# Full attention: rows in pairs from both ends, router groups of scattered tiles, masked value sums at the front of a batch

## The reference

```python
q, k, v = jnp.split(jnp.einsum('bsd,df->bsf', x, W), 3, axis=-1)
scores = jnp.einsum('bqd,bkd->bqk', q, k) / jnp.sqrt(jnp.float32(d_k))
scores = jnp.triu(scores, k=0)
scores = jnp.where(scores == 0, MASK_NEG, scores)
attn = jax.nn.softmax(scores, axis=-1)
return jnp.einsum('bqk,bkd->bqd', attn, v)
```

## Time and profile before

| | us |
|---|---|
| median of three runs | 1553.63 |
| lowest and highest of them | 1550.43, 2271.89 |
| time of the profiled execution | 1557.52 |
| its span, first to last instruction | 1555.8 |
| PE, DVE, ACT, POOL busy | 1285.8, 1052.4, 905.6, 778.7 |
| full attention, from its first projection to the last x | 1056.6 to 1315.1 |
| rest of the second routing, up to its last slots | 1315.1 to 1334.4 |

### The profile page before, as it was taken

The page is one execution under the profiler, slowest core; times in us unless marked ns, Lnnn a source line. Parts: engine busy times, 40 slices in busy tenths (PEclk is TensorE's granted clock), DMA queues, the critical chain, the costliest instruction groups (busy, mean ns, idle before and its releaser), DMA issues. The chain is left out here.

```text
span 1555.8 us, 34583 instructions
## 1 busy us (share of the span) xinstructions
PE 1285.8 (83%) x9684; PEld 1011.7 (65%) x9684; DVE 1052.4 (68%) x3673; ACT 905.6 (58%) x2301; POOL 778.7 (50%) x812
## 2 busy tenths in 40 slices
PE   3999999999999999999963888809978885288890
PEld 2677766766776666766743888805765665288890
DVE  7566877878777776877754555566886788355563
ACT  2677768777776776767642444406765664144450
POOL 3566676685866768567562444500022422435451
PEclk9899999999999999999985999959998998599996
DMA  8999990000000000000013122130000000121215
GB/s 255 210 207 207 208 167 8 4 12 1 15 0 6 10 0 15 0 7 8 0 56 108 56 60 59 45 108 1 1 14 15 25 16 16 45 58 57 62 54 162
DMA packets 129396, 91.89 MB, mean 59 GB/s; under 512 B 9115, under 2 KB 122030, under 8 KB 128992
## 3 DMA queue, kind: packets, MB, share of 16 engines
q1 hardware_dynamic: 118080, 71.84, 21.6%
q0 software_dynamic: 9248, 16.94, 3.3%
q10 hardware_dynamic: 1920, 1.60, 0.3%
HBM read 30.86 MB, written 61.64 MB: 59 GB/s over the span
## 5 line engine op out<-in xcount | busy, mean ns | idle before, releaser
L905 DVE CUSTOM_DVE_ANT_0 sc<-ps,mask 128x256 f32<-128x256 f32 x518 | 199.2, 421 | 159.4 <-PE ps L720 137.1
L827 ACT ACTIVATE sc<-sc,mx 128x256 f32<-128x256 f32 x516 | 256.9, 501 | 38.8 <-DVE mx L905 38.2
L1055 POOL TENSOR_TENSOR rot<-rot,sin 128x512 f32<-128x512 f32 x132 | 183.6, 1391 | 185.9 <-DVE rot L914 185.9
L1202 POOL DMA_INDIRECT yt<-yo,xt x160 | 160.4, 1002 | 197.9 <-DVE yo L1302 169.4
L534 POOL DMA_INDIRECT xg<-r_xw,r_slot x128 | 126.6, 989 | 170.0 <-DVE r_slot L511 137.9
L835 ACT COPY pT<-pt 128x512 f32<-128x512 f32 x257 | 150.1, 584 | 104.0 <-PE pt L730 95.7
L720 PE MATMUL ps<-K,Q 64*128 64x256 f32 x1036 | 193.3, 436 | 14.7 <-DVE mx L905 14.7
L1262 ACT ACTIVATE hT<-ph,b 128x256 f32<-128x256 f32 x320 | 125.4, 475 | 87.0 <-PE ph L1225 87.0
L730 PE MATMUL pt<-ident,sc 128*128 128x128 f32 x1028 | 170.7, 289 | 1.8 <-ACT sc L827 1.6
L743 PE MATMUL po<-pT,V 128*64 128x128 f32 x2048 | 170.7, 288 | 0.0
L730 PEld LDWEIGHTS pt<-ident,sc 128*128 128x128 f32 x1028 | 109.3, 142 | 86.6 <-issue 58.5
(11 more groups left out here) (235 smaller groups left out, 2730.3 us busy)
## 6 DMA issues: line engine op xcount, KB each, us to landing
xg<-zeros SPq DMA_DIRECT2D x76, 520.0 KB, 9.9
xt<-xg SPq DMA_DIRECT2D x80, 130.0 KB, 2.1
got<-yt SPq DMA_DIRECT2D x32, 256.0 KB, 4.4
yt<-yo,xt POOLq DMA_INDIRECT x160, 2.3
xg<-r_xw,r_slot POOLq DMA_INDIRECT x128, 2.3
w<-in_w SPq DMA_DIRECT2D x1, 2048.0 KB, 8.1
out_x<-x SPq DMA_DIRECT2D x8, 256.0 KB, 4.3
x<-in_hidden SPq DMA_DIRECT2D x6, 256.0 KB, 8.2
```

Source lines behind the costliest of these rows:

```text
L827: nc.scalar.activation(sc[:, b, h, :], sc[:, b, h, :], ACT.Exp, scale=-1.0, bias=mx[:, b, h:h + 1], accum_out=ls[:, c % 2, b, h:h + 1]).th ...
L905: nc.vector.tensor_tensor_reduce(sc[:, b, h, :], ps[:, h, 0:2 * P], (mask0 if b == 0 else mask)[:, :], -float(HD) ** -0.5, 3e38, ALU.add, ...
L1055: nc.gpsimd.tensor_tensor(rot[:, which, :], rot[:, which, :], s.sin[:, pos(sb)], ALU.mult).then_inc(S["pool"], 1)
L1202: nc.gpsimd.indirect_dma_start(out=s.yt, out_offset=bass.IndirectOffsetOnAxis(ap=xt[:, k, r, HID:HID + 1].bitcast(U32), axis=0), in_=yo[:, ...
```

## The change

The rows of a batch are taken in the order 0, 15, 1, 14, ..., 7, 8. A row's place in that order is r, its tile i; buffers, signals and `first` go by r, keys and x by i. A pair has five chunks. The router's groups are four tiles that are neighbours in this order (for group 0 the tiles 0, 15, 1, 14), so `Router` gets a list of tiles and ids of its own, which POOL writes with 16 `iota` instructions ahead of the stage's other work; DVE waits for them. `ROUTE_AT` becomes 11, 21, 31, 42, 51, 61, 71, 81.

The masked sums are no longer made row by row. Four matmuls of 512 columns (`a` from 12 to 15) give the column sums of all tiles of V, and DVE adds them up into `pre[:, i, :]`, one place per tile, after its first six takes. Their counts are constants set by memset. `finish` loses its add and reads `pre[:, i, :]`; `oo` gets two buffers. The scores of the first seven chunks stand between the projections and these matmuls and behind a wait for all of V. The third and fourth of the matmuls wait until DVE has read the bank (`pre` signal). The next batch's projections wait for that signal instead of the last add.

```diff
+        order = [i for k in range(BTILES // 2) for i in (k, BTILES - 1 - k)]
+        ids = m.sb("ids_b", [P, TOPK, TILES], U32)
+        rt = Router(nc, m, s, 3, 2, 0, [b * BTILES + i for b in range(BATCH) for i in order], ids)
...
-        ROUTE_AT[3], ROUTE_AT[7] = NCH + 5, 2 * NCH + 2
+        ROUTE_AT[3], ROUTE_AT[7] = NCH + 2, 2 * NCH + 1
...
-                for a in range(12):
+                for a in range(16):
...
+                    if 10 <= a < 14:
+                        pe.wait_ge(S["v"], START + 4 * b + a - 9)
+                    if a >= 14:
+                        pe.wait_ge(S["pre"], START + 4 * b + a - 13)
                     if a < 2:
-                        pe.wait_ge(S["pre_sb"], START + (BTILES - 1) * b)
+                        pe.wait_ge(S["pre"], START + 4 * b)
+                    if a == 12:
+                        pe.wait_ge(S["v"], START + 4 * (b + 1))
+                        for g in range(AHEAD):
+                            scores(g)
...
+                    elif a >= 12:
+                        g = a % 4 * SB_TILES
+                        ins = nc.tensor.matmul(pp[:, a % 2, :], s.ones[:, :], V[:, g:g + SB_TILES, 0:HID],
+                                               start=True, stop=True)
...
-                    i, c, _, _ = chunk[g]
-                    if c == 0 and i > 0:
-
-                        pe.wait_ge(S["pre_sb"], START + (BTILES - 1) * b + max(i - 2, 0))
-                        nc.tensor.matmul(pp[:, i % 2, 0:HID + 1], s.ones[:, :], V[:, i - 1, :], start=True,
-                                         stop=True).then_inc(S["pre"], 1)
...
+                def sums(a):
+
+                    dve.wait_ge(S["proj"], START + 16 * b + a + 1)
+                    for t in range(SB_TILES):
+                        i = a % 4 * SB_TILES + t
+                        if i < BTILES - 1:
+                            ins = nc.vector.tensor_tensor(pre[:, i + 1, 0:HID], pre[:, i, 0:HID],
+                                                          pp[:, a % 2, t * P:(t + 1) * P], ALU.add)
+                            ch.link(ins)
+                    dve.sem_inc(S["pre"], 1)
...
+                    nc.vector.scalar_tensor_tensor(oo[:, r % 2, :], pre[:, i, :], st[:, r % UBUF, 2:3],
+                                                   po[:, r % 2, 0:HID + 1], ALU.mult, ALU.add).then_inc(S["o"], 1)
...
                 for g in range(AHEAD - 1):
                     take(g)
+                for a in range(12, 16):
+                    sums(a)
...
+            for b in range(BATCH):
+                for k in range(TOPK):
+                    for t in range(SB_TILES):
+                        i, step = order[t], order[t + SB_TILES] - order[t]
+                        nc.gpsimd.iota(ids[:, k, bass.ds(b * BTILES + t, BTILES // SB_TILES, step=SB_TILES)].bitcast(I32),
+                                       pattern=[[step * P, BTILES // SB_TILES]],
+                                       base=(k * TILES + b * BTILES + i) * P, channel_multiplier=1).then_inc(S["ids"], 1)
```

More of the change, by code:

```diff
@@ L100 @@
     "norm1": ROUTE + " high", "experts1": EXPERT,
-    "norm2": NORM + " xT", "full": "proj qk v s copy u bias p w0 t pt pv pre pre_sb o chain tri",
+    "norm2": NORM + " xT", "full": "proj qk v s copy u bias p w0 t pt pv pre ids o chain tri",
     "norm3": ROUTE, "experts3": EXPERT,
@@ L348, with __init__ @@
     LINKS = 30
-    def __init__(self, nc, m, s, tag, bufs, primed):
+    def __init__(self, nc, m, s, tag, bufs, primed, tiles=None, ids=None):
         self.nc, self.s, self.S, self.nth, self.bufs, self.primed = nc, s, s.signals[f"norm{tag}"], tag // 2, bufs, primed
+        self.tiles, self.ids = tiles, s.ids if ids is None else ids
         small = [P, SB_TILES, EXPERTS]
@@ L1361, in full_stage @@
         block = ctx.enter_context(nc.Block())
-        chunks = [[(k, min(4, BTILES - k)) for k in range(i, BTILES, 4)] for i in range(BTILES)]
-        first = [sum(len(c) for c in chunks[:i]) for i in range(BTILES + 1)]
+        rows = [(i, [(k, min(4, BTILES - k)) for k in range(i, BTILES, 4)]) for i in order]
+        first = [sum(len(chunks) for _, chunks in rows[:r]) for r in range(BTILES + 1)]
         NCH = first[-1]
-        MARKS = 4 * BTILES + NCH
-        chunk = [(i, c, k0, n) for i in range(BTILES) for c, (k0, n) in enumerate(chunks[i])]
+        MARKS = 4 * BTILES + BTILES - 1 + NCH
+        chunk = [(r, i, c, k0, n) for r, (i, chunks) in enumerate(rows) for c, (k0, n) in enumerate(chunks)]
         def at(b, g, step):
@@ L1426, in _ @@
                     ins.then_inc(S["proj"], 1)
[L1427 to L1434, removed]
                 def turn(g):
-                    i, c, k0, n = chunk[g]
+                    r, i, c, k0, n = chunk[g]
                     pe.wait_ge(S["p"], START + NCH * b + g + 1)
@@ L1545, in _ @@
             nc.vector.memset(V[:, :, HID:], 1.0)
+            nc.vector.memset(pre[:, 0, :], 0.0)
+            for i in range(1, BTILES):
+                nc.vector.memset(pre[:, i, HID:], float(i * P))
             dve.wait_ge(S["tri"], START + 2)
+            dve.wait_ge(S["ids"], START + BATCH * TOPK * SB_TILES)
             rt.start(dve)
@@ L1595, in take @@
                                                 ALU.mult).then_inc(S["bias"], 1)
[L1597 to L1613, removed]
-                    ins.then_inc(S["o"], 1)
-                    dve.wait_ge(S["o"], START + BTILES * b + i + 1)
-                    ch.link(nc.vector.reciprocal(st[:, i % UBUF, 3:4], oo[:, HID:]))
@@ new lines, in finish @@
+                def finish(r):
+                    i = rows[r][0]
+                    dve.wait_ge(S["pv"], START + NCH * b + first[r + 1])
+                    dve.wait_ge(S["w0"], START + BTILES * b + r + 1)
+                    nc.vector.scalar_tensor_tensor(oo[:, r % 2, :], pre[:, i, :], st[:, r % UBUF, 2:3],
+                                                   po[:, r % 2, 0:HID + 1], ALU.mult, ALU.add).then_inc(S["o"], 1)
+                    dve.wait_ge(S["o"], START + BTILES * b + r + 1)
+                    ch.link(nc.vector.reciprocal(st[:, r % UBUF, 3:4], oo[:, r % 2, HID:]))
@@ L1628, in _ @@
                     route(b, g)
-                for i in range(chunk[NCH - 2][0], BTILES):
-                    finish(i)
-                assert ch.n == MARKS
+                for r in range(chunk[NCH - 2][0], BTILES):
+                    finish(r)
+                assert ch.n == MARKS, ch.n
             for g in range(NCH, NCH + MORE):
```

63 lines of the change are left out of this document (31 added, 32 removed).

## The result

The changed kernel takes 1578.3 us (median; 1577.6 to 1581.1), the kernel before 1553.2 in the same set of runs: ratio 1.0171, 95% interval 1.0151 to 1.0191, 25 us more. (One of the four runs of the kernel before was a slow one, 2271.9 us, and is not in the ratio.) Forecast were 12.5 more. The direction holds and the time lies 0.7 us inside the top of the range (1546 to 1579), but the forecast size is half of what came, and the main case's own range (1559 to 1573) doesn't hold it.

What follows compares the result with a forecast made beforehand. DVE was taken to bound the stage, with 25.8 us of waits to win. Waits +10.6, work moved in +4.8, tail -4.9 and scores +2.0 gave +12.5 on 1553.6, so 1566.1 us, range 1546 to 1579.

Steps and rivals of the forecast that it cites:

- main case: Whole kernel: DVE waits of 30 to 42 us, time 1559 to 1573 us; chance 0.52.
- the sum: DVE waits 36.4 against 25.8, work moved in +4.8, tail -4.9, scores +2.0: together +12.5 us.
- work moved in: Batches: later steps of group 2 enter batch 0, group 6's enter batch 1; +4.8 us of DVE work.
- tail: Last x to last slots: only group 7 is left, 14.4 us instead of 19.3, so -4.9 us.
- fronts and the wait for V: Batch fronts: first scores wait for all of V and start about 1 us later per batch; +2.0 us.
- The iotas: Prologue: sixteen GpSimd iotas end before the copies of V, costing 0 us; uncovered, 4.8 us once.
- Rival A: Batches: order does what balance promises, a group costs DVE 1.7 us of waits; -8.3 us, 1545.3 us; chance 0.20.
- Rival B: Batches: order changes nothing, DVE's waits stay 25.8 us; +1.9 us, 1555.5 us; chance 0.22.
- Rival C: Router groups: TensorE's clock stays low from root to slots, 21 us more in seven groups; 1587 us; chance 0.06.
- part 3: Router groups: stops of TensorE at root and counts, with low clock, make DVE wait; 34.4 us with 1.0 at fronts.
- Part 4: Batch fronts: six chunks of lead cover the late first transposition; low clock costs 1 us a batch, 2.0 us.
- Level pairs: Row pairs between groups: DVE 9.1 and PE 9.3 us a pair are level, leaving 0.3 us of waiting.

Runs made afterwards that it cites:

- e14: Changed kernel plus three unused TensorE matmuls (fillers) at the router groups' roots only, none at the counts; ratio to before 1.0069, stage 288.6 us.
- e1: Changed kernel with rows in natural order and groups at the old steps, keeping front sums and wait for V; ratio to before 1.0069, stage 290.5 us.
- e12: e1 plus unused filler matmuls: four ahead of the third sum matmul, others at roots and counts; ratio to before 1.0017, stage 279.1 us.
- e5: Changed kernel with third and fourth sum matmuls and their adds moved to steps 2 and 3; ratio to before 1.0130, stage 297.7 us.
- e7: Changed kernel plus three unused filler matmuls at each group's root and at most counts; ratio to before 1.0056, stage 284.8 us.
- e8: Changed kernel with the router's root made on DVE instead of ScalarE; ratio to before 1.0274, stage 316.9 us.

## Why the prediction was right in direction and wrong in size

**The sum term by term.** Inside the batches DVE waited 49.1 us, where the sum has 36.4. Counted from the statistics of one group to those of the next, it waited 6.1, 7.5, 5.7 and 7.3 us in groups 0, 1, 4 and 5, together 26.7 where 22.4 were forecast; 5.6 in group 3 (3.8); 14.1 in groups 2 and 6 with the ends of the batches (7.2); 2.7 ahead of the first statistics of both batches (1.0 + 2.0). The waits of before were 24.4 us inside the batches and not 25.8: the prediction counted the two of 0.8 us ahead of the first takes in. So the waits grew by 24.7 us where 10.6 were forecast, and these 14.1 us are the miss; the other terms came as forecast: work moved in 4.5 (4.8), tail -5.2 (-4.9), fronts and the wait for V 1.9 (2.0). The iotas took 1.34 us and ended at 1051.3, seven us ahead of the first copy of V: 0, as said.

**What was right.** The mechanism at each place: PE idle in two parts ahead of the first transposition (3.92 and 0.28 us, though 5 were asked for), 3.4 to 4.05 us ahead of the counts of groups 0, 1, 3, 4 and 5, low clock after each, and last x to last slots in 14.1 us (14.4). The batches, at 125.2 and 137.6 us, are each some 5 us above the 120 and 132 that were to show it right. Rival A had the right idea of the order by itself, 1.0 and 2.5 us a batch, and the wrong one of its groups. Rival B falls with the 24.7 us of added waits. Rival C's mechanism did not come: the clock recovers within a group, for some 10 us between root and counts. That the range holds the time is luck: its top was drawn for C, and the main case's waits of 30 to 42 us and its 1573 us are both passed. A fall lasts 81.6 / 14 = 5.8 us, 40.5 / 8 = 5.1 before, as I had read; it is mostly their number that grew.

**The step that failed** is in part 3: what the stop at a root costs with the low clock behind it. I took "some 2 us of waits" from a group's statistics to its counts, and 1 us at the root of groups 2 and 6. DVE waited 3.0, 4.1, 3.0 and 3.9 us there in groups 0, 1, 4 and 5, and 3.6 in groups 2 and 6 each. That is 11 us of the 12.7 by which the waits exceed 36.4. The counts, where I had put the second fall, took 3.1, 3.5, 2.8 and 3.5 us, no more than the 3.6 that the sum's 5.6 a group leaves for them. With fillers at the roots alone (e14) the waits ahead of the counts are 1.8, 2.8, 1.8 and 2.8 us, those at the roots of groups 2 and 6 1.4, the waits inside the batches are 33.8 us (36.4 in the sum), and the stage is 288.6 - 277.6 = 11.0 us longer than before, close to the forecast 12.5. So the sum gives the time of a kernel whose roots bring no low clock.

**How much of the 25.9 is the clock's.** Fillers take 18.7 us off the changed kernel and 4.4 off the one before, so 14.3 us are the clock's and 284.8 - 273.2 = 11.6 remain. That 11.6 lies near the forecast too, but by luck: the forecast was made against a kernel with its eight falls. e1 and e12 split both parts. The sums in front, in natural order, bring 11.4 - 4.4 = 7.0 us of the clock's part and 5.9 of the rest; the order with its groups brings 18.7 - 11.4 = 7.3 and 5.7. Part 4 had put 2.0 us on the clock behind the fronts, and nothing for what a later start does to the falls further on. The falls could have been counted ahead (two fronts, seven roots, five counts), but not priced from before: a us of low clock was worth 0.16 us there, 0.24 in e1, 0.27 in the changed kernel. Level pairs (PE 9.3, DVE 9.1 us a pair) can't be the whole reason, as e1 has natural order; why it costs more once the sums stand in front isn't shown.

**Two smaller ones.** The ends of the batches: behind the root of group 2 (and 6) PE runs at the lower level for 10.2 us, and DVE, with few chunks or none left to take, waits for each row; 7.1 us a batch in place of 3.6, 4.9 with fillers, of which 3.5 for the last values (2.6) is not the clock's. And part 4 let six chunks of lead cover a first transposition 5.3 us later; it came 6.4 us later, and some 2.9 a batch of that reached the end in the new order (e5), while in natural order (e1, falls included) the batches grew by 5.6. That PE, which behind the front needs as much time as DVE or more, wins nothing back is my reading.

The Trainium skill ("TensorE: Matmul & The Clock Gate", section "HAM oscillation — how this bites in real kernels") counts the extra time of a throttled stretch as half its length. By that, as an estimate, e7's 69 us would be worth 34.5; the stage got 18.7. PE was busy in 73 of the changed kernel's 82 us of low clock, so its idle time explains little of the difference; most of the rest did not reach the stage's end. The rule of the Trainium skill, in the same section, that work behind each long gap restarts cold, named ahead of the result for the fronts, agrees with this trace but for a delay: behind the gap of 3.92 us in batch 0 the clock was 0.89 in the first whole us and 0.50 in the next, behind that of 3.93 in batch 1 it was 0.50 from the first.

**What stays open.** Of the 11.6 us that remain with the clock up, e12 gives 5.9 to the sums and the wait for V (2 of it is that wait) and 5.7 to the order with its groups. The 5.7 hold e7's two falls at the fronts, which e12 has filled; which row pattern causes the rest wasn't tried. A timeline with the clock up and no added matmuls can't be made, so the fillers' own time on PE is in every such number.

## What to carry to other kernels

Price each stop of TensorE with the slow stretch behind it, and count the stops: half of this change's loss was the clock's, with fourteen falls for eight, and the view of waits shows it only as DVE waiting for scores. Where TensorE must stand for 3 to 4 us, a few matmuls that nobody needs, placed in the gap, gave 18.7 us of 303.5 back; in the kernel before they gave 4.4 of 277.6, so the worth of a us of low clock has to be measured in the kernel at hand. An order that is better by itself (1.0 and 2.5 us a batch) can lose once other work is laid into it. That the level pairs took away a lead which had covered the disturbances is a reading of this, not shown.

## What the runs showed of the hardware

- The lower level holds on while PE works without a pause: in group 1 PE was busy 5.88 of the 5.90 us from 1138.1 to 1144.0 at a mean of 0.58.
- Whether a gap between 2.3 and 3.2 us is followed by a fall can't be told from its length: 2.30 us was (in batch 1 of the changed kernel), 2.37 in batch 0 of before wasn't, and with one filler a good third of the low time went. Gaps filled down to 1.1 to 1.8 us were not followed by one in batch 0 of e7 (0.99); in its batch 1 two of the seven filled gaps were, with 1.49 and 1.61 us of idle left.
- ACT's root with its two table loads cost DVE little by itself: without it (e8) the waits were 50.1 us for 52.9.
- Tiny DVE instructions on 128x4 took 0.16 us each, 0.2 chained; e8's eleven more a group, for a reciprocal less, made its stage 13.4 us longer.
